# PSUM banks by stage, three batches for the choice of experts, later first weights and a joint power in a cross-attention and mixture-of-experts kernel

## What is computed

```python
x = x + cross_attention(layernorm(x), ctx)          # 16 heads, 77 keys
ln1 = layernorm(x) * ln1_w + ln1_b                  # block, "S" = sequences' tokens
q, k, v = split(ln1 @ qkv_weight.T)                 # 16 query heads, 4 key heads
h1 = x + causal_attention(q, k, v) @ proj.T
z2 = layernorm(h1) * ln2_w + ln2_b
probs = softmax(z2 @ router_weight)
top_p, top_i = top_k(probs, 2); top_p /= sum(top_p)
order = argsort(top_i.reshape(-1), stable=True)     # place of a token in its expert
within = place; valid = within < 1280               # capacity 1.25 * N * 2 / 8
out = h1 + scatter_add(top_p * (gelu(z2[e] @ w1[e]) @ w2[e]))
```

## Time and profile before

| | before |
|---|---|
| median of three runs | 1679.21 us (1679.16 to 1680.63) |
| profiled execution | 1678.78 us, of which the traced span is 1677.0 |
| mean granted clock | 0.959 |
| PE busy | 1520.7 us (91%) |
| DVE, ACT, POOL busy | 951.9, 713.4, 837.0 us |

### The profile page before, as it was taken

How to read it: one execution, slowest core, us unless ns; L and a number is a source line. 1 busy time by engine, 2 the same in 40 slices (tenths; PEclk the granted TensorE clock), 3 DMA queues, 4 the chain that set the end, 5 groups by cost and what they waited for, 6 DMA issues and landing times. The chain is left out here.

```text
span 1677.0 us, 30921 instructions
## 1 busy us (share of the span) xinstructions
PE 1520.7 (91%) x11103; PEld 1325.8 (79%) x11104; DVE 951.9 (57%) x1780; ACT 713.4 (43%) x1448; POOL 837.0 (50%) x953
## 2 busy tenths in 40 slices
PE   7788788999999999998863999899999979999986
PEld 5566677888888888877752989899999869899975
DVE  4766656777777767677756445543233555343361
ACT  2343443555554455455435434433332534343341
POOL 1343444556655556678741637453343665463242
PEclk9999889999999999999975999999999989999999
DMA  6111211122222212222211424343442533442221
GB/s 240 39 51 58 70 51 51 46 76 77 71 67 67 66 63 72 69 95 79 80 57 55 102 57 105 75 110 68 90 89 41 110 98 76 97 102 51 36 40 23
DMA packets 63597, 124.58 MB, mean 74 GB/s; under 512 B 13232, under 2 KB 13648, under 8 KB 62921
## 3 DMA queue, kind: packets, MB, share of 16 engines
q1 hardware_dynamic: 45184, 92.54, 16.9%
q0 software_dynamic: 17920, 29.31, 10.4%
q10 hardware_dynamic: 328, 0.50, 0.1%
HBM read 89.02 MB, written 46.27 MB: 81 GB/s over the span
## 5 line engine op out<-in xcount | busy, mean ns | idle before, releaser
L1351 PEld LDWEIGHTS hidden_ps<-gT,w 128*128 128x128 f32 x2880 | 350.4, 192 | 9.1 <-ACT hT L1270 4.2
L1351 PE MATMUL hidden_ps<-gT,w 128*128 128x256 f32 x2880 | 352.7, 284 | 5.3 <-ACT hT L1270 3.2
L1380 PE MATMUL expert_ps<-w,hT 128*128 128x512 f32 x1440 | 341.7, 397 | 8.1 <-DVE og L1320 8.1
L1380 PEld LDWEIGHTS expert_ps<-w,hT 128*128 128x128 f32 x1440 | 272.4, 191 | 65.9 <-DVE og L1320 8.5
L1295 DVE TENSOR_TENSOR hT<-gl,hT 128x512 fp32r<-128x512 f32 x160 | 130.5, 824 | 250.4 <-ACT hT L1270 250.3
L1155 POOL TENSOR_TENSOR w<-raw,w 128x1024 fp32r<-128x1024 f32 x64 | 155.0, 2433 | 201.2 <-ACT w L1149 200.8
L1268 ACT ACTIVATE gl<-hidden_ps 128x512 f32<-128x512 f32 x160 | 95.7, 598 | 335.3 <-PE hidden_ps L1351 312.6
L1252 POOL DMA_INDIRECT out_dram<-og,idx x80 | 130.3, 1628 | 153.7 <-DVE og L1320 140.0
L1320 DVE TENSOR_SCALAR og<-expert_ps,kept 128x512 f32<-128x512 f32 x80 | 59.1, 749 | 159.0 <-PE expert_ps L1380 154.9
L1278 ACT ACTIVATE gT<-yk 128x256 fp32r<-128x256 f32 x160 | 66.9, 418 | 109.1 <-DVE yk L1306 107.3
L1024 PE MATMUL main_ps<-wqkv_hi,zT 128*128 128x512 f32 x256 | 109.0, 441 | 4.8 <-DVE h L798 4.8
(11 more groups left out here) (178 smaller groups left out, 3225.6 us busy)
## 6 DMA issues: line engine op xcount, KB each, us to landing
raw<-L_ffn_moe_w_dram SPq DMA_DIRECT2D x64, 512.0 KB, 3.6
normed_tokens<-h SPq DMA_DIRECT2D x128, 65.0 KB
xa<-x_dram SPq DMA_DIRECT2D x32, 256.0 KB, 2.7
xc<-x_dram SPq DMA_DIRECT2D x32, 256.0 KB, 3.0
attended_rows<-x SPq DMA_DIRECT2D x32, 256.0 KB, 2.0
fx<-attended_rows SPq DMA_DIRECT2D x128, 64.0 KB
out_dram<-fx SPq DMA_DIRECT2D x128, 64.0 KB
fx<-qkv_rows_dram SPq DMA_DIRECT2D x1, 1536.0 KB, 6.6
```

The source lines that it names most:

```text
L1351: last = pe.matmul(pH[:, q, f * W:(f + 1) * W], w1[p][l][:, k, cols], xT[g.s % 2][r][:, k, :], start=k == 0 and n == 0, stop=k == KT - 1 a ...
L1380: last = pe.matmul(pY[:, k, :], hT[par][l][:, f, k * P:(k + 1) * P], w2[p][r][:, f, :], start=f == 0 and n == 0, stop=f == FT - 1 and n == 2)
```

## The change

In steps below 14 each kind of PSUM job has a bank of its own: the four groups of transposes of softmax weights take banks 0 to 3, q takes 0 and 1, xt 4, wo 5, val 6 and pv 7. A job that takes bank 0 or 1 from the scores waits for the first of the two `shifted` events.

The choice of experts is made in three batches instead of six: 28 tiles in step 48, 3 in step 50, the last at the end; `choose` stands at the head of DVE's step and not at its end, and `count_places` stays a step later. The first expert's pieces of weights are loaded in steps 38, 40, 42, 44, 46, 47, 48 and 49 instead of 38 to 45. On DVE `tops` and `gap` stand behind L879 and the four L883. On POOL the two powers of a tile's statistics become one of two columns, with the wait for the old `h0` ahead of it. ACT makes 4 of 8 rows in a group of the table, and DVE 4. At the start ACT copies wq_hi before it issues four loads, and copies the token selectors in step 2.

```diff
@@ -51,7 +51,7 @@
 BATCH = 8
-BY_ACT = 6
+BY_ACT = 4
 
@@ -161,9 +161,11 @@
 EARLY_LOW = FF
+OWN_BANKS = {"pt": 0, "q": 0, "xt": 4, "wo": 5, "val": 6, "pv": 7}
 LATE = NT + LP + 2
-CHOICES = ((LATE, 0, 9), (LATE + 2, 9, 18), (LATE + 6, 18, 24), (LATE + 10, 24, 28), (STEPS - 2, 28, 31),
-           (STEPS, 31, 32))
+FIRST_PIECES = {LATE: (0,), LATE + 2: (1,), LATE + 4: (2,), LATE + 6: (3,), LATE + 8: (4,), LATE + 9: (5,),
+                LATE + 10: (6,), LATE + 11: (7,)}
+CHOICES = ((STEPS - 4, 0, 28), (STEPS - 2, 28, 31), (STEPS, 31, 32))
 PASSES = ((0, 0), (0, 1), (1, 0))
@@ -205,7 +207,9 @@
         for kind, t, j, half in psum_jobs(i):
-            if kind == "s":
+            if i < FF and kind in OWN_BANKS:
+                take((kind, t, j), [OWN_BANKS[kind] + j])
+            elif kind == "s":
                 take((kind, t, j), [0, 1, 2, 3])
@@ -235,7 +239,7 @@
     token_mask = sb("token_mask", [TB, 16 * TB], F32R)
-    expo = sb("expo", [P, 1])
+    expo = sb("expo", [P, 2])
     fx = sb("fx", [P, FX, D])
@@ -273,7 +277,7 @@
     wx, wf, wh = sb("wx", [P, 1]), sb("wf", [P, 2]), sb("wh", [P, 1])
-    rx, rf, rff, rh = sb("rx", [P, 2]), sb("rf", [P, 8]), sb("rff", [P, 2]), sb("rh", [P, 2])
+    rx, rf, rh = sb("rx", [P, 2]), sb("rf", [P, 8, 2]), sb("rh", [P, 2])
     shift = sb("shift", [P, 8])
@@ -321,7 +325,10 @@
             for old, t_old, j_old in ousted[kind, t, j]:
-                pe.wait_ge(*read_out[old](t_old, j_old))
+                if old == "s" and kind != "s" and place[kind, t, j] < 2:
+                    pe.wait_ge(s["shifted"], 2 * t_old + 1)
+                else:
+                    pe.wait_ge(*read_out[old](t_old, j_old))
 
@@ -421,9 +428,9 @@
                     sp.dma_start(choice["product"][:, 0:3 * P], a["routing_orders"]).then_inc(const_in, 16)
-                if 0 <= i - LATE < CH:
+                for j in FIRST_PIECES.get(i, ()):
                     sp.wait_ge(s["x2_done"], NT)
-                    weights["load"](sp, 0, 0, 0, i - LATE)
+                    weights["load"](sp, 0, 0, 0, j)
             for f in range(NT - FX, NT):
@@ -504,13 +511,12 @@
                     var = mvf[:, f % 2, 1:2]
-                    link(pool, "pool_link", linked,
-                         pool.tensor_scalar(wf[:, 0:1], var, 1.0 + EPS, EPS * EPS, ALU.mult, ALU.add))
-                    pool.tensor_tensor(rff[:, f % 2:f % 2 + 1], wf[:, 0:1], expo[:, 0:1], ALU.pow)\
-                        .then_inc(s["rstd_f"], 1)
+                    pool.tensor_scalar(wf[:, 0:1], var, 1.0 + EPS, EPS * EPS, ALU.mult, ALU.add)
+                    link(pool, "pool_link", linked, pool.tensor_scalar(wf[:, 1:2], var, EPS, None, ALU.add))
                     need(pool, s["h0_done"], f - 7)
-                    link(pool, "pool_link", linked, power(rf[:, f % 8:f % 8 + 1], var, wf[:, 1:2]))
-                    pool.tensor_scalar(shift[:, f % 8:f % 8 + 1], mvf[:, f % 2, 0:1], rf[:, f % 8:f % 8 + 1], -1.0,
+                    pool.tensor_tensor(rf[:, f % 8, :], wf[:, :], expo[:, :], ALU.pow).then_inc(s["rstd_f"], 1)
+                    pool.wait_ge(s["rstd_f"], f + 1)
+                    pool.tensor_scalar(shift[:, f % 8:f % 8 + 1], mvf[:, f % 2, 0:1], rf[:, f % 8, 1:2], -1.0,
                                        ALU.mult, ALU.mult).then_inc(s["shift_f"], 1)
@@ -523,18 +529,18 @@
                     pool.memset(groups["xg"][:, :, :, :], 0.0).then_inc(s["xg_cleared"], 1)
-                if 0 <= i - LATE - 1 < CH:
-                    weights["low"](pool, 0, 0, i - LATE - 1)
+                for j in FIRST_PIECES.get(i - 1, ()):
+                    weights["low"](pool, 0, 0, j)
             pool.wait_ge(s["xg_cleared"], 1)
...
         def _(act):
+            act.wait_ge(wq_in, 16)
+            act.activation(wq[0][:, :, :], rq, ACT.Copy).then_inc(s["wq_hi"], 1)
             act.dma_start(x2[0:TB, 0, 0:P], a["token_sel"]).then_inc(tok_in, 16)
...
             act.dma_start(bo[:, :], a["L0_xattn_bo"].partition_broadcast(P)).then_inc(bias_in, 16)
-            act.wait_ge(wq_in, 16)
-            act.activation(wq[0][:, :, :], rq, ACT.Copy).then_inc(s["wq_hi"], 1)
             for i in range(STEPS):
@@ -542,7 +548,7 @@
                         .then_inc(s["xt_hi"], 1)
-                if i == 1:
+                if i == 2:
                     act.wait_ge(tok_in, 32)
@@ -588,7 +594,7 @@
                     act.activation(h1[:, f % 4, 0:D], fx[:, f % FX, :], ACT.Identity, bias=shift[:, f % 8:f % 8 + 1],
-                                   scale=rf[:, f % 8:f % 8 + 1]).then_inc(s["h0_done"], 1)
+                                   scale=rf[:, f % 8, 1:2]).then_inc(s["h0_done"], 1)
                 f = tile(i, FF + 2)
@@ -640,8 +646,8 @@
                         .then_inc(s["consts_done"], 1)
-                if 0 <= i - LATE - 1 < CH:
-                    weights["high"](act, 0, 0, i - LATE - 1)
+                for j in FIRST_PIECES.get(i - 1, ()):
+                    weights["high"](act, 0, 0, j)
             act.wait_ge(s["found"], 1)
@@ -791,6 +797,9 @@
                     low_halves(i)
+                batch = chosen(i, 0)
+                if batch is not None:
+                    choose(*batch)
                 f = tile(i, FF + 4)
@@ -859,12 +868,6 @@
                     dve.reciprocal(rec2[:, f % 2, :], den2[:, :]).then_inc(s["rec2_done"], 1)
-                f = tile(i, FF + 5)
-                if f is not None:
-                    dve.wait_ge(s["lg_evac"], f + 1)
-                    chained(dve.max(tops[:, f, :], logits[:, f, :]))
-                    need(dve, s["gap_exp"], f)
-                    dve.tensor_tensor(gap[:, :], tops[:, f, 1:2], tops[:, f, 0:1], ALU.subtract).then_inc(s["gap"], 1)
                 t = tile(i, 2)
@@ -883,6 +886,12 @@
                     k_turn.then_inc(s["k_turned"], 1)
+                f = tile(i, FF + 5)
+                if f is not None:
+                    dve.wait_ge(s["lg_evac"], f + 1)
+                    chained(dve.max(tops[:, f, :], logits[:, f, :]))
+                    need(dve, s["gap_exp"], f)
+                    dve.tensor_tensor(gap[:, :], tops[:, f, 1:2], tops[:, f, 0:1], ALU.subtract).then_inc(s["gap"], 1)
                 f = tile(i, FF - 1)
@@ -904,11 +913,8 @@
                     need(dve, s["zt_mm"], f)
-                    dve.tensor_scalar(z, fx[:, f % FX, :], mvf[:, f % 2, 0:1], rff[:, f % 2:f % 2 + 1],
+                    dve.tensor_scalar(z, fx[:, f % FX, :], mvf[:, f % 2, 0:1], rf[:, f % 8, 0:1],
                                       ALU.subtract, ALU.mult).then_inc(s["z_done"], 1)
-                batch = chosen(i, 0)
-                if batch is not None:
-                    choose(*batch)
             last_tile(CHOICES[-1][1])
@@ -1081,7 +1087,7 @@
                "is_blk": sb("is_blk", [P, 2, BATCH, NBLK], F16), "hot_blk": sb("hot_blk", [P, 2, BATCH, NBLK], F16),
-               "equal": sb("equal", [P, 9, E]), "hot": sb("hot", [P, 2, NT, E]), "rest": sb("rest", [P, NT, E]),
+               "equal": sb("equal", [P, NT, E]), "hot": sb("hot", [P, 2, NT, E]), "rest": sb("rest", [P, NT, E]),
                "product": sb("product", [P, 2 * NT * E]), "empty": sb("empty", [P, NBLK]),
```

## The result

The changed kernel takes 1711.8 us (median of four runs, 1707.5 to 1712.8) against 1679.9: 1.0184 times the time before, with a 95% interval of 1.0165 to 1.0203. The direction was the one forecast, the size was not: +32 us where +9.5 was worked out, and above the range's end of 1701. The profiled execution took 1712.81, its span 1710.8, so the trace to explain is 33.8 us longer than the one before.

The account below looks back on a forecast made before the run. PE was taken as nearly gapless in joint steps, with POOL and DVE partly setting the late pace. Terms -5.4 + 9.1 + 1.2 + 3.0 + 6.0 - 4.4 = +9.5 gave 1688.3, median 1688.7; range 1668 to 1701.

Parts of the forecast that it names:

- What bounds, and the mechanism: Whole kernel: PE nearly gapless in joint steps; late tops and gap delay POOL's weighing, the power behind it, z and PE.
- the gap doesn't reach PE: Rival, at POOL's power for z: it is ready in time anyway, 15.4 and 9.1 leave the sum; 1664, chance 0.12.
- Late gap in joint steps: Steps with cross-attention and block attention together: z's followers start .70 later in each of 13 steps; +9.1, bounds 0 and +13.
- Joint power: POOL's two powers as one of two columns: +.05 for some 23 steps; +1.2, ends 0 and +13.
- Late steps: Block attention alone: late gap +15.4, clock +1.6, batches and counts leaving -14.0; +3.0, bounds -4 and +14.
- The link: Late steps: delay from late gap over POOL's weighing and power to z's transposes, from T+4.24 to T+5.92; +1.68 a step.
- one more drop: Late steps: the wait of 2.3 before z's transposes pulls PE's granted clock down once more; +1.6.
- The clock rival: Late steps: the clock falls behind each of eight waits for z, +8, counts at half clock +3.5; 1700, chance 0.20.
- Own banks: Steps below 14: transposes stop waiting for oT_lo, but q still waits for xT_lo; -5.4, bounds -3 and -9.
- Tail: Last steps: batch of 28 tiles +2.3, its counts before the last router matmul +5.8, three-tile batch -2.1; +6.0, bounds +3 and +11.
- Table: Experts' row table, ACT making 4 of 8 rows: eight groups each .55 to .6 shorter; -4.4, bounds -2 and -5.
- The range: Whole kernel time: 1668 to 1701 over forecast and rivals; the forecast's own is 1683 to 1694.

Follow-up runs that it names:

- e1: The changed kernel with tops and gap early again on DVE, ahead of the query and key transposes; 1669.2 us (0.9945 of the kernel before).
- e4: The kernel before with the late tops and gap alone; 1706.9 us (1.0172).
- e10: The changed kernel with the power of z's layernorm moved ahead of the weighing on POOL; 1676.4 us (0.9978 of the kernel before).
- e3: The changed kernel with both edits undone: tops and gap early again, two powers of one column; 1662.4 us (0.9900 of the kernel before).
- e2: The changed kernel with two powers of one column again, tops and gap still late; 1697.6 us (1.0136 of the kernel before).
- e6: The kernel before with the joint two-column power alone; 1.0036, +6.7 us by the medians.
- e7: The kernel before with the three batches of choices and the first weights over twelve steps; 0.9940, -8.9 us by the medians.
- e9: The changed kernel with nine added matmuls, results unused, in PE's waits for z in steps 38 to 45; 1698.7 us.
- e14: The changed kernel with the nine added matmuls again, repeated beside the changed kernel on one chip; 1699.2 us (1.0118 of the kernel before).
- e5: The kernel before with a bank of its own for each stage in steps below 14; 0.9980, -3.2 us by the medians.
- e11: The kernel before with ACT making 4 of 8 rows of the table and DVE 4; 0.9970, -3.0 us.
- e8: The changed kernel with early gap, two powers, and the count of 28 tiles split into PE's waits in steps 48 and 49; 1656.0 us.

## Why the prediction was right in its sign and short by 23 us

- **What bounds, and the mechanism**: right. The late gap reaches PE through POOL's order (e1, e4, e10), and the other parts together are a gain (e3). The rival "the gap doesn't reach PE" would have been 1664, and e1, with the gap early, is at 1669.
- **Late gap in joint steps**: the term that failed first. Forecast .70 in each of 13 steps, +9.1, of which .20 was for the joint power's second tensor_scalar; measured 1.05 (from +3.9 to +17.5 over steps 19 to 32), +13.6. The chain was right to 0.2 up to the end of the weighing. The gap alone cost .71 to .73 a step (e2, e4) and not .50. The power's end came .46 later behind the weighing and not .20, for two tensor_scalars, a link and two columns; behind the late gap .34 of that is paid in each step (the changed kernel against e2).
- **Joint power**: the most mis-sized term. +.05 in 23 steps, +1.2, was taken from the wrong question, how long two columns take (0.73 for 0.56). Not asked was what the power that goes had been covering: z now collides with L455 (L448 in e6) in the steps before the first weighing. From step 14 to 19 the difference grows by 6.0 in the changed kernel, by 5.6 in e6 and by 0.8 in e2, which has two powers. Behind the late gap come the 4.4 of the joint steps and 2.9 in the late ones (h1 of tile 16 to that of tile 29: 203.3 us against 200.4 in e2): 12 to 13 in all by these rows, where the joint power alone cost 6.7 (e6).
- **Late steps**: forecast +3.0, measured +12.5 (from 17.5 to 30.0). The waits of the batches went as read (h 4.8 to none). Each part alone came out near its term, in part by luck, as the clock is in what they measured: from h1 of tile 16 to that of tile 29 e7 takes 15.9 less than the kernel before (forecast 14.0) and e4 15.8 more (forecast 15.4). Together they are no sum. The link is 6.32 - 4.24 = 2.08 per step instead of 1.68, some 3.6 us over nine steps. The rest is the clock: I reckoned one more drop, +1.6, though the same text worked out a wait over 2 us in eight steps; e9 and e14 give 6.6 to 6.7 for it. By the clock's record in the traces it falls five times in that stretch, where it fell twice before, and some 24 us of it are at 1.2 GHz and not 7. It is the late gap that does this, and not the joint power: the stretch in e3 and in e2, which differ in the late gap alone, columns as in the earlier trace rows:

```profile
648.00:824.00 176.00, 169.66 (x1078) 142.52 (x1076) 130.24 (x261) 94.52 (x219) 134.82 (x207) 1.00 0.23 77
657.00:857.00 200.00, 178.52 (x1059) 150.96 (x1058) 128.32 (x260) 92.15 (x217) 131.73 (x206) 0.93 0.20 68
```

  PE idles 6.3 us in e3 and 21.5 in e2, 15.1 more, which is about the wait that was forecast; the other 9 us are the same work at a lower clock. Without the late gap the batches' going had left no drop at all; with it they came back. The clock rival had the right cause and, without the other two terms, 1700.
- **Own banks**: forecast -5.4, e5 -3.2. q waits for xT_lo, as said. The gain of the odd steps was overrated, as earlier transposes move the layernorm of x beside POOL's addition of bo: eleven of them (42.4 to 205) take 12.2 us in e5 and 10.0 before. In step 11 of the changed kernel, DVE and POOL:

```profile
169.36 1.26 POOL L491 TENSOR_TENSOR xc<-xc,bo 128x512 f32<-128x512 f32 x1
169.43 1.93 DVE L683 TENSOR_SCALAR xa<-xa,mvx,rx 128x512 f32<-128x512 f32 x1 [0.99 <-POOL rx L445]
```

- **Tail**: right, +6.0 against 5.9 (30.0 to 35.9). One operation of the batch of 28 took 2.01 beside POOL's low piece and one 1.25 beside L495, the others .39 to .42.
- **Table**: right. -4.4 against -4.7 (35.9 to 31.2), a group now being bound by DVE (L750 .82, L754 .69 and L757 like L750); e11 alone shows 3.0 by medians, 5.0 by its ratio. Behind the table the trace has another +2.6 that no part touches, where e9's trace has -1.0. The table's groups in the changed kernel, for the earlier trace rows:

```profile
L750 DVE TENSOR_TENSOR is_blk<-ramp,blk 128x640 f16<-128x640 f16 x8 | 6.6, 819 | 0.0
L663 ACT ACTIVATE hot_row<-distance,consts 128x512 f16<-128x512 f16 x8 | 5.8, 722 | 0.3
L754 DVE TENSOR_TENSOR hot_row<-ramp,row 128x512 f16<-128x512 f16 x8 | 5.5, 685 | 0.0
```

- **The range**: it was the sum of terms that were each sized by themselves. The three that were short (power, joint, clock) hang on the late gap: it makes the power's later end count in the joint steps (0.1 us without it, 4.4 with it), and its wait pulls the clock. So the late gap costs 28 alone (e4), 35 beside the other parts without the joint power (e2 less e3) and 42 beside all of them (changed kernel less e1), by the medians; the sum had 24.5 for it.

## What to carry to other kernels

When an operation is moved later on one engine, follow it to the engine that consumes it in order, and ask what stands behind it there: two small DVE operations moved by 2 us held back five on POOL, a power, z and PE. When an operation is taken away, ask what its time had kept apart, and not only what it took. A wait on PE of the size met here, 2.6 us in eight steps, is paid twice, once for itself and once for the clock of what follows; PE work that is due anyway can be put into such waits (e8).

## What the runs showed of the hardware that I had not expected

- DVE's z took 1.45 instead of 0.54 us when POOL's L448 had started some 0.05 earlier, in five steps of e6 (14 to 18); the seven of steps 13 to 19 averaged 1.23 against 0.57. The layernorm of x took 1.93 beside L491 and the memset behind it, where it takes .54 alone.
- POOL's power of two columns takes 0.72 to 0.73, of one 0.55 to 0.57 in most places (up to 0.84 in some); the weighing's two tensor_scalars of eight columns take 0.32 and 0.41 at the median, the one of one column 0.22.
- Nine added matmuls in each of eight waits of 2.6 us made a kernel 6.7 us faster by the rows of its late steps, with the granted clock at 0.99 instead of 0.94.
- The same program up to step 38 reached step 20 at times 5 us apart in two executions, so a difference of two profiled executions is not yet a difference of kernels.
